# A two-layer graph block on one Trainium2 core: another order for the set-up, parts stored singly, six row transfers a half

## The reference

```
h = max(layernorm(x), 0)
x = x + L0(h, adj)      # masked softmax attention, 8 heads of 16, with W_qkv, b_qkv, W_out, b_out
h = max(layernorm(x), 0)
x = x + L1(h, adj)

L0: q, k, v = split(h @ W_qkv + b_qkv)
    y = softmax(where(adj, q @ k.T / sqrt(16), -inf)) @ v ;   return y @ W_out + b_out
L1: z_l, z_g, v = h @ Wl, h @ Wg, h @ Wv
    A_l = max(cosine(z_l, z_l), 0),  A_g = exp(-|z_g - z_g'|^2 / 2), both with a zero diagonal and times adj
    K = 0.9 * A_l / rowsum(A_l) + 0.1 * A_g / rowsum(A_g) ;   return (K @ v) @ Wo
```

## Time and profile before

| | us |
|---|---|
| median of three runs | 919.57 |
| the profiled execution | 919.7 |
| its span | 917.9 |
| TensorE busy | 835.4 (91%) |
| VectorE busy | 718.6 (78%) |
| ScalarE busy | 528.1 (58%) |
| GpSimd busy | 350.7 (38%) |
| first score tile starts | 40.69 |
| its first maximum starts | 41.31 |
| time outside the span | 1.8 |

### The profile page before, as it was taken

The page is one execution under the profiler, slowest core; times in us unless marked ns, Lnnn a source line. Parts: engine busy times, 40 slices in busy tenths (PEclk is TensorE's granted clock), DMA queues, the critical chain, the costliest instruction groups (busy, mean ns, idle before and its releaser), DMA issues.

```text
span 917.9 us, 15562 instructions
## 1 busy us (share of the span) xinstructions
PE 835.4 (91%) x4947; PEld 482.5 (53%) x4947; DVE 718.6 (78%) x2081; ACT 528.1 (58%) x1217; POOL 350.7 (38%) x416
## 2 busy tenths in 40 slices
PE   1479899999999999999999999999999999999976
PEld 0323345646464654646465554656465564646465
DVE  2777869788887979788797879888797978877435
ACT  1117585655647475665757575565758565575731
POOL 4424452443434253353525244353525334332310
PEclk9859999999999999999999999999999999999989
DMA  1322303031111203021120303021120303000000
GB/s 51 115 74 60 99 18 99 13 93 37 63 54 48 81 30 99 14 80 49 39 78 31 99 30 91 22 71 46 48 81 31 99 13 94 25 1 13 1 12 12
DMA packets 65536, 48.48 MB, mean 53 GB/s; under 512 B 10672, under 2 KB 65456, under 8 KB 65456
## 3 DMA queue, kind: packets, MB, share of 16 engines
q1 hardware_dynamic: 65456, 47.48, 17.2%
HBM read 30.28 MB, written 16.78 MB: 51 GB/s over the span
## 4 chain that ended last, share of the span: by engine, by line
PE 79%; DVE 11%; issue 4%; ACT 3%; POOL 1%; DMA 1%; SPq 1%; DVEq 0%; ACTq 0%; POOLq 0%
PE adj L578 12%; PE pv L571 12%; PE adj L583 12%; PE score L545 12%; PE turned L557 11%; PE turned L556 8%; PE work L589 5%; PE work L578 3%; DVE scrap L753 3%; PE work L653 2%; PE work L671 1%; DVE rbf_arg L785 1%; DVE zgT_parts L873 1%; DVE max_parts L761 1%; DVE zlT_parts L878 1%
## 5 line engine op out<-in xcount | busy, mean ns | idle before, releaser
L753 DVE CUSTOM_DVE_ANT_0 scrap<-score,mask_add 128x512 f32<-128x512 f32 x512 | 337.8, 684 | 45.3 <-PE score L545 41.4
L895 ACT ACTIVATE probs_t<-turned 128x512 f32<-128x512 f32 x512 | 293.5, 596 | 128.3 <-PE turned L557 125.9
L445 POOL TENSOR_TENSOR probs_t<-probs_t,keep_t 128x512 int32<-128x512 int32 x128 | 170.5, 1332 | 259.1 <-ACT probs_t L895 259.1
L545 PE MATMUL score<-qk_rows 96*128 96x512 bf16 x512 | 202.2, 397 | 12.3 <-DMA qk_rows<-split_dram 8.6
L557 PE MATMUL turned<-qk_rows 99*128 99x512 bf16 x512 | 195.7, 382 | 0.0
L556 PE MATMUL turned<-bar_t,ident_b 128*128 128x512 bf16 x384 | 147.1, 383 | 9.1 <-ACT probs_t L895 9.0
L571 PE MATMUL pv<-probs_t,v_cols 128*32 128x512 f32 x1024 | 136.4, 605 | 0.0
L545 PEld LDWEIGHTS score<-qk_rows 96*128 96x128 bf16 x512 | 50.0, 98 | 121.0 <-issue 74.1
L929 ACT ACTIVATE rbf_exp<-rbf_arg,rbf_bias 128x512 f32<-128x512 f32 x64 | 46.2, 722 | 63.1 <-DVE rbf_arg L785 63.1
L557 PEld LDWEIGHTS turned<-qk_rows 99*128 99x128 bf16 x512 | 50.6, 99 | 44.3 <-issue 1.2
L583 PEld LDWEIGHTS adj<-z,adj_cos 128*128 128x128 f32 x512 | 66.5, 190 | 11.2 <-DVE adj_cos L776 1.6
(11 more groups left out here) (114 smaller groups left out, 1198.3 us busy)
## 6 DMA issues: line engine op xcount, KB each, us to landing
qk_rows<-split_dram SPq DMA_DIRECT2D x384, 64.0 KB, 2.2
split_dram<-split SPq DMA_DIRECT2D x32, 384.0 KB, 2.4
x_sb<-in_x_dram SPq DMA_DIRECT2D x16, 256.0 KB, 2.9
out_dram<-out_sb SPq DMA_DIRECT2D x16, 256.0 KB, 2.3
qk_rows<-max_rows SPq DMA_DIRECT2D x96, 4.0 KB, 1.8
adj_sb<-in_adj_dram SPq DMA_DIRECT2D x1, 256.0 KB, 3.4
wqkv_sb<-in_L_gnn_W_qkv_dram SPq DMA_DIRECT2D x1, 192.0 KB, 2.7
bias_v<-in_L_gnn_b_qkv_dram SPq DMA_DIRECT2D x1, 64.0 KB, 2.9
```

What stands on the lines that cost most here:

```text
L445: pool.tensor_tensor(tile, tile, keep_t[:, w // HG % T, :], ALU.mult).then_inc(probs_masked.sem, 1)
L545: pe.matmul(score_bank[u % 2][:, :], qk_rows[0:ROWS, b % 2, 0, h, t * P:(t + 1) * P], qk_rows[0:ROWS, b % 2, 1, h, :], start=True, stop=Tr ...
L753: dve.tensor_tensor_reduce(scrap[:, u % 2, :], score_bank[u % 2][:, :], mask_add[:, u % T, :], -1.0, 3.0e38, ALU.add, ALU.min, neg_max[:, ...
L895: act.activation(probs_t[:, k % 4, w % HG, :], turned_bank[w % 2][:, :], ACT.Exp, scale=SCALE).then_inc(probs_ready.sem, 1)
```

## The change

1. SP loads adj before the two broadcast biases, on a signal of its own (`s_adj_loaded`).
2. DVE takes the moments first, then splits the q and k weights and casts adj, all before `hT_split`. The early waits for `s_qkv_loaded` on PE, POOL and ACT go.
3. ACT runs an exponential on a 128x4 tile (`table_warm`) at the start.
4. PE turns the masks in two pieces: two banks before q, two after k. ACT makes `mask_t` and `bar_t` from each bank after `k_hi`; DVE makes `keep_t`, after ACT has read the bank. The weights are folded after v.
5. The first k goes to `pv_bank`, so it doesn't wait for q's readers. Its middle and low parts are made by DVE, not by POOL. `resid` has a buffer for q and one for k, in all batches.
6. The ones in `qk_rows` are written by POOL after the first `x_biased`.
7. In all batches the six parts are stored one by one, each when it is ready, to a `split_dram` laid out [which, part, 16 features, 8 heads, 512]; the rows of a half come in 6 transfers (48, 48, 32, 32, 16 and 16 rows), where those for q read a part three times or twice.

```diff
+Q_RUNS = ((0, 3), (1, 2), (2, 1))
+K_RUNS = (3, 2, 1)
...
-        resid = sb("resid", [P, N])
+        resid = sb("resid", [P, 2, N])
...
-        split_dram = nc.dram_tensor("split_dram", (2, 3, P, N), BF16, kind="Internal").ap()
+        split_dram = nc.dram_tensor("split_dram", (2, 3, DH, H, N), BF16, kind="Internal").ap()
...
+        def qk_bank(batch, which):
+
+            return pv_bank if (batch, which) == (0, 1) else work_bank
...
-                for which, parts in enumerate((Q_PARTS, K_PARTS)):
-                    for block_row, part in enumerate(parts):
-                        src = split_dram[which, part, h0 * DH:(h0 + HG) * DH, :]
-                        sp.dma_start(
-                            qk_rows[block_row * DH:(block_row + 1) * DH, batch % 2, which, h0:h0 + HG, :],
-                            src.rearrange("(h f) n -> f h n", f=DH)).then_inc(rows_loaded[half].sem, 16)
...
+                for (part, times), parts in zip(Q_RUNS, K_RUNS):
+                    src = split_dram[0, part:part + 1, :, heads, :]
+                    load(0, times * DH, src.broadcast_to([times, DH, HG, N]).rearrange("c f h n -> c f (h n)"))
+                    load(1, parts * DH, split_dram[1, 0:parts, :, heads, :].rearrange("c f h n -> (c f) (h n)"))
...
-                    for which in range(2):
-                        reached(sp, lo_ready, b, which + 1)
-                        reached(sp, hi_ready, b, which + 1)
-                        sp.dma_start(split_dram[which].rearrange("c f n -> f c n"),
-                                     split[:, which, :, :]).then_inc(split_stored.sem, 16)
+                    for part in range(3):
+                        for which in range(2):
+                            if part == 0:
+                                reached(sp, hi_ready, b, which + 1)
+                            elif part == 1:
+                                second_made(sp, b, which)
+                            else:
+                                parts_made(sp, b, which)
+                            sp.dma_start(split_dram[which, part].rearrange("f h n -> h f n"),
+                                         split[:, which, part, :]).then_inc(split_stored[which].sem, 16)
...
+                        if (b, which) == (0, 1):
+
+                            reached(dve, rest_ready, 0, 2)
+                            dve.tensor_copy(split[:, 1, 1, :], resid[:, which, :]).then_inc(first_mid.sem, 1)
+                            reached(dve, first_mid, 0)
+                            dve.tensor_tensor(split[:, 1, 2, :], resid[:, which, :], split[:, 1, 1, :],
+                                              ALU.subtract).then_inc(first_lo.sem, 1)
...
+            act.wait_ge(s_blank.sem, 1)
+            act.activation(table_warm[:, :], minus_half[:, :], ACT.Exp)
...
+                for m, src in enumerate(score_bank + turned_bank):
+                    act.wait_ge(s_adj_turned.sem, m + 1)
+                    act.copy(mask_t[:, m, :], src[:, :])
+                    act.activation(bar_t[:, m, :], src[:, :], ACT.Identity, bias=bar_bias[:, 0:1],
+                                   scale=BIG).then_inc(s_masks.sem, 1)
```

## The result

The changed kernel takes **915.58 us** (median of 22 runs, 912.49 to 918.53), the kernel before on the same chips 920.8 (22 runs). The ratio is **0.9948, 95% interval 0.9935 to 0.9961**. It is faster, by 5 us instead of 11.3, and the time lies above the range. The profiled execution took 914.57, with a span of 912.8.

The account below looks back on a forecast made before the run. PE was taken to bound the middle, so the gain had to come from the start: the first maximum at 30.0 instead of 41.3 gains 11.3 us, and 919.7 falls to 908.4 us. Range: 904.6 to 912.3.

Parts of the forecast that it names:

- The path to the stores: Start of the kernel up to the last store of q and k parts: 11.7 us earlier, at 19.1 instead of 30.83.
- The landing of 2.45 I leave as it is: Last store of the parts: takes 2.45 us to land, as before, so parts are in DRAM at 21.5.
- The next x: Load of 256 KB issued ahead of the row transfers, at 19.4, before the last part has landed: costs nothing.
- I take the middle, 29.2: First half's rows arrive at 29.2, between 26.0 (transfers land in 2.2 us as before) and 32.5 (few DMA engines).
- The price of the rows: Time from the first issue of the first half's row transfers until the rows are there: 7.7 us.
- upper bound of 11.0: First half's row transfers if one DMA engine carries 156 KB: 9.0 us plus 2.0 for the way, rows at 32.5.
- The DVE side: DVE before the first maximum: POOL's fill holds the `wz_parts` cast to 26.5, DVE free at 28.9, hidden by rows at 29.2.
- Later batches: Stores and row transfers after batch 0 cost nothing: a half has 18.4 us until used, so even 11 us fits.
- The clock: Low stretch of the clock around the first tiles: same stretch, moved forward, with an error of about 1 us.
- rival 5: PE's clock stays low one slice (23 us) longer, costing up to 11 us: 917 to 919 us; chance 0.03.
- 1 us earlier there is 1 us off the end: First masked maximum on DVE: its gain carries fully to the end, since PE has no slack in the middle; 11.3 us.
- Rival 1: Few DMA engines carry the row transfers: rows at 30.8 to 32.5, total 910.0 to 911.7, named 910.8 us; chance 0.32.

Follow-up runs that it names:

- halves apart: Changed kernel, but in batch 0 the second half's row transfers are issued only when the first half has landed: 913.8 us, ratio 0.9925.
- feature outer: Changed kernel with rows of `qk_rows` ordered feature, then copy, so all six row transfers have outermost extent 16: 911.55 us, ratio 0.9891.
- k on 3 and 2: Changed kernel with a padding row behind each part in DRAM, so k's reads also have outermost extents 3 and 2: 932.46 us, ratio 1.0134.
- PE kept busy: "feature outer" with the `wz_parts` cast on ACT, stores on 16 engines and 66 unread matmuls in PE's set-up waits: 910.72 us, ratio 0.9889.

## Why the prediction was wrong

- **The path to the stores: right.** Moments 3.52 (3.7), `x_norm` 8.21 (8.2), q 12.95 (12.9), the last store issued by 19.07 (19.1). Beside DVE's casts `ln_shift` took 1.00 instead of 0.20 and `rstd` 1.37 instead of 1.05: 1.1 lost, as put in. That it came out to a tenth is partly luck, as `x_norm` began anywhere from 8.2 to 8.9 in the other versions of the changed kernel. Two errors cancelled: the subtraction for k's low part took 1.52 beside POOL's, not 0.7, and k's product 0.99 at the full clock, not 1.65.
- **"The landing of 2.45 I leave as it is": wrong by 0.8.** It was 3.21, and the parts were in DRAM at 22.3, not 21.5. The new stores, with an outermost extent of 8, ran at a share of 0.46 to 0.52, as 8 of 16 engines would; on 16 the last needed 1.70, and the row transfers could be issued 1.3 us sooner. The next x, which I put at nothing, was issued at 20.20 while that store was in flight; what it cost no run shows.
- **"I take the middle, 29.2": the step that failed.** The rows came at 34.74. The price of the rows was 7.7, and they took 12.4. Of the 5.5 us, 0.8 are the landing above; 3.1 are the choice of the middle, as the first half alone took 10.8 ("halves apart"), against an upper bound of 11.0; 1.6 are the second half, which I had left out of the sum although its transfers are issued right behind, to the same engines. So even the bound was too low for the kernel as it is. That the first half alone met it is partly luck: an engine ran at about 22 GB/s, the rate that gave 7.3 and not 9.0, but it had 16 KB of the next x to carry besides, and the way there and back took 2.8 instead of 2.0. The Trainium skill, "DMA: Bandwidth & Descriptors", section "Why a DMA increments its semaphore by 16 and not by 1", has the rule (the largest number up to 16 that divides the outermost extents), and the shares of 0.18 and 0.13 agree with it, as do the versions with copies inside ("feature outer") and with k on 3 and 2. Two outcomes lay before me, all engines or few; a middle between two mechanisms is a value that neither gives. The rule had said which of them, and I gave it 0.32.
- **The DVE side: right, without effect.** Fill 20.17 to 27.09 (19.4 to 26.4), cast ended at 27.3 (26.5), DVE free at 29.7 (28.9). All are 0.8 late for one reason, the fill's later start: `x_resid` took 1.71 where I put 1.26, beside DVE, and began 0.3 late.
- **Later batches: nearly right.** "Even the upper bound of 11 fits" held but for one wait of PE in front of a score tile, 1.8 at 107.69. With k on few engines as well it no longer held.
- **The clock: right.** It was low from 22 to 63 us, so up to 28.0 after the first tile, against 28.3 before: the same stretch, moved forward, and rival 5 did not come.
- **"1 us earlier there is 1 us off the end": right within a microsecond here, not in general.** 5.70 at the first maximum, 6.26 at the last layer norm, 5.1 at the end. Over the versions the way from the first tile to the last layer norm differs by up to 4, and goes with the clock's low stretch.
- **Rival 1** named the mechanism and gave 910.8. It is the one that came, 4 to 5 us dearer.

## What to carry to other kernels

Before cutting the number of DMA transfers, look at the outermost extent of each one as the hardware gets it: a copy or part index in front turned 16 engines into 3 and 2, and the order "feature, then copy" brought them back with the same six transfers and the same bytes. Watch the DMA share in the stretch before the wait ends: 0.19 and 0.12 in a stretch where everything waits were three and two engines at work here. When a cost has two mechanisms, take one of them and price the other, with everything that is queued behind it.

## What the runs showed of the hardware

- Reads from DRAM into 16 rows of `qk_rows` each, in 1 KB pieces, did not get faster by being pushed harder: one queue moved 138 GB/s at a share of 0.46, and two queues 127 at 1.18.
- POOL's fill of 6.92 us held DVE's cast from f32 to fp32r for 4.52, while ACT did the same cast beside the fill in 0.51, and DVE's reads of PSUM ran under the fill at their usual length (two of `keep_t` in 1.27, one alone 0.68 in the kernel before).
- In "PE kept busy" the granted clock held at 1.00 through 22 to 32, with PE busy for 6.4 of 10 us, and fell to 0.50 in the microsecond from 32 on, after PE had stood for 2.69 us ahead of the first tile and then followed DVE's maxima.
